# Last four hidden tiles transposed by TensorE, the first rests taken with a negated identity, and every queue reordered

## The reference

```python
def fp4_quant_dequant(x):                  # blocks of 16 along the last dim
    scale = jnp.maximum(jnp.max(jnp.abs(xb), -1, keepdims=True) / 6.0, 1e-12)
    idx = jnp.searchsorted(_MID, jnp.abs(xb / scale))
    return _GRID[idx] * jnp.sign(xb / scale) * scale
gate, y = fp4_linear(x, w_gate), fp4_linear(x, w_up)
h = silu(gate) * y
return fp4_linear(h, w_down)
x = layernorm(x + attn(x)); x = layernorm(x + ffn(x))
```

## Time and profile before

| | us |
|---|---|
| median of 3 runs | 320.72 (320.18 to 323.29) |
| the profiled execution, whole | 319.53 |
| its span, first to last instruction | 317.8 |
| TensorE, VectorE, ScalarE, GpSimd busy | 299.8, 278.9, 223.8, 241.5 |
| mean granted TensorE clock | 0.982 |

### The profile page before, as it was taken

How to read it: one execution, slowest core, us unless ns; L and a number is a source line. 1 busy time by engine, 2 the same in 40 slices (tenths; PEclk the granted TensorE clock), 3 DMA queues, 4 the chain that set the end, 5 groups by cost and what they waited for, 6 DMA issues and landing times.

```text
span 317.8 us, 6470 instructions
## 1 busy us (share of the span) xinstructions
PE 299.8 (94%) x1911; PEld 271.1 (85%) x1911; DVE 278.9 (88%) x725; ACT 223.8 (70%) x545; POOL 241.5 (76%) x258
## 2 busy tenths in 40 slices
PE   6949999999999989999999999999999999999783
PEld 2939988999899879889999998999999998899682
DVE  4996699969999999999988996989998899998953
ACT  7582986679677488669785886686877758587563
POOL 2897886476968967896978889487998757769671
PEclk9996999999999999999999999999999999999979
DMA  6704011832637446433562269338463273267601
GB/s 223 279 35 134 1 68 34 140 74 86 185 75 121 92 86 144 157 95 98 150 180 75 65 107 198 88 104 151 103 120 84 67 112 84 71 136 130 77 33 66
DMA packets 38722, 34.36 MB, mean 108 GB/s; under 512 B 25760, under 2 KB 31776, under 8 KB 38688
## 3 DMA queue, kind: packets, MB, share of 16 engines
q1 hardware_dynamic: 32064, 22.81, 34.5%
q10 hardware_dynamic: 6624, 11.15, 11.1%
HBM read 22.87 MB, written 5.18 MB: 88 GB/s over the span
## 4 chain that ended last, share of the span: by engine, by line
PE 67%; POOL 9%; issue 7%; DVE 7%; DMA 6%; ACT 3%; SPq 1%; ACTq 0%; POOLq 0%; DVEq 0%
PE ps L2160 15%; PE ps L2161 15%; PE ps L2164 15%; PE ps L2173 5%; PE ps L2174 5%; PE ps L2170 5%; DMA h_gT<-h_g 4%; POOL h_q L504 3%; DMA w_pair<-in_w_attn_dram 2%; PE ps L2224 2%; POOL h_n L485 1%; DVE hqT_lo L1584 1%; PE ps L2269 1%; POOL pr_lo L445 1%; PE ps L2283 1%
## 5 line engine op out<-in xcount | busy, mean ns | idle before, releaser
L2160 PE MATMUL ps<-guT_hi,xqT_hi 128*128 128x512 f32 (+1 forms) x192 | 74.0, 385 | 1.5 <-ACT xqT_hi L822 1.4
L2161 PE MATMUL ps<-guT_lo,xqT_hi 128*128 128x512 f32 (+1 forms) x192 | 72.1, 375 | 0.0
L504 POOL TENSOR_TENSOR h_q<-h_gT,h_sT 128x768 f32<-128x768 bf16 x30 | 51.8, 1731 | 12.3 <-DVE hqT_lo L1584 10.7
L2164 PE MATMUL ps<-guT_hi,xqT_lo 128*128 128x512 f32 (+1 forms) x192 | 56.5, 375 | 0.0
L485 POOL TENSOR_TENSOR h_n<-w_raw,h_rs 128x704 f32<-128x704 f32 x32 | 47.1, 1473 | 9.0 <-DVE h_rs L1414 8.9
L2160 PEld LDWEIGHTS ps<-guT_hi,xqT_hi 128*128 128x128 f32 x192 | 36.1, 188 | 6.8 <-ACT xqT_hi L822 1.7
L445 POOL TENSOR_TENSOR pr_lo<-pr,pr_hi 128x512 fp32r<-128x512 f32 (+3 forms) x32 | 28.5, 901 | 16.8 <-ACT pr_hi L791 16.8
L2164 PEld LDWEIGHTS ps<-guT_hi,xqT_lo 128*128 128x128 f32 x192 | 35.5, 188 | 6.0 <-DVE xqT_lo L1521 0.2
L2161 PEld LDWEIGHTS ps<-guT_lo,xqT_hi 128*128 128x128 f32 x192 | 36.1, 188 | 4.5
L2160 PE MATMUL ps<-dnT_hi,hqT_hi 128*128 128x256 f32 x160 | 39.6, 283 | 0.0
L2161 PE MATMUL ps<-dnT_lo,hqT_hi 128*128 128x256 f32 x160 | 39.5, 283 | 0.0
(11 more groups left out here) (130 smaller groups left out, 852.1 us busy)
## 6 DMA issues: line engine op xcount, KB each, us to landing
h_sT<-h_scales_dram SPq DMA_DIRECT2D x30, 384.0 KB
out_dram<-wq_gu ACTq DMA_DIRECT2D x31, 128.0 KB, 1.8
xs<-in_x_rows_dram ACTq DMA_DIRECT2D x7, 512.0 KB, 4.6
x_full<-in_xt_rows_dram ACTq DMA_DIRECT2D x6, 512.0 KB, 3.7
w_raw<-in_w_ffn_dram SPq DMA_DIRECT2D x6, 352.0 KB, 6.0
h_scales_dram<-h_s SPq DMA_DIRECT2D x30, 32.0 KB, 2.6
w_pair<-in_w_attn_dram SPq DMA_DIRECT2D x1, 512.0 KB, 5.1
x_full<-in_xt_rows_dram SPq DMA_DIRECT2D x1, 512.0 KB, 3.5
```

The source lines that it names most:

```text
L504: nc.gpsimd.tensor_tensor(h_q[:, p, :], h_gT[:, p, :, :].rearrange("p c t -> p (c t)"), h_sT[:, p, :], ALU.mult).then_inc(h_quant, 1)
L2160: nc.tensor.matmul(dst, lh, rh, start=(first and i == 0), stop=False)
L2161: nc.tensor.matmul(dst, lh, rl, start=False, stop=False)
L2164: last = nc.tensor.matmul(dst, ll, rh, start=False, stop=(end and i == len(terms) - 1))
```

## The change

Three things. Tiles 28 and 29 take TensorE's way too, so the DMA way ends with tile 27 (the counts in `h_transpose`, `h_round` and `h_divisors` shift by two). The rests of v and of the quantised x of sequence 0 are no longer subtracted on VectorE: TensorE subtracts the high part in PSUM with the negated identity and ScalarE copies the rest. And the five queues are written out in another order, with other banks and other waits for them; the first of sequence 0's scores stand ahead of `combine`.

```diff
-        h_at = {30: (7, 5), 31: (4, 3)}
+        h_at = {28: (7, 6), 29: (7, 3), 30: (7, 6), 31: (7, 3)}
...
+            def v_remainder(n, u):
+                act.wait_ge(v_left, 2 * n + u + 1)
+                c = slice(2 * u, 2 * u + 2)
+                nc.scalar.copy(v_lo[:, c, :].rearrange("p i d -> p (i d)"), ps[:, v_at[n][u], :]).then_inc(v_lo_ready, 1)
...
+            def xq_remainder(n, u):
+                act.wait_ge(xq_left, 2 * n + u + 1)
+                c = slice(D * u, D * (u + 1))
+                nc.scalar.copy(xqT_lo[:, :, c], ps[:, xq_at[n][u], :].rearrange("p (c t) -> p c t", c=DK)).then_inc(xqT_lo_ready, 1)
...
             def v_rest(n, u):
                 dve.wait_ge(v_hi_ready, 2 * n + u + 1)
+                if n == 1 and u == 0:
+                    dve.wait_ge(v_lo_ready, 2)
...
+            def v_subtract(n, u):
+                c = slice(2 * u, 2 * u + 2)
+                pe.wait_ge(v_hi_ready, 2 * n + u + 1)
+                nc.tensor.matmul(ps[:, v_at[n][u], :], neg_ident[:], v_hi[:, c, :].rearrange("p i d -> p (i d)"), start=False,
+                                 stop=True, skip_group_check=True).then_inc(v_left, 1)
...
+            def xq_subtract(n, u):
+                c = slice(D * u, D * (u + 1))
+                pe.wait_ge(xqT_hi_ready, 2 * n + u + 1)
+                nc.tensor.matmul(ps[:, xq_at[n][u], :], neg_ident[:], xqT_hi[:, :, c], start=False, stop=True,
+                                 skip_group_check=True).then_inc(xq_left, 1)
```

More of the change, by code:

```diff
@@ L630, in _ @@
             x_dequant(4, 1)
+            out_stats(9, 1)
+            p_rest(5, 1)
             h_spread(13, 1, 7)
[L632 removed]
+            p_rest(5, 2)
+            h_normalise(16, 0)
+            p_rest(5, 3)
+            h_spread(14, 0, 8)
             x_stats(5, 0)
[L634 to L636 removed]
+            x_rest(6, 0)
+            out_stats(10, 0)
+            x_rest(6, 1)
             x_normalise(5, 0)
[L638 removed]
@@ L2364, in _ @@
-            reads(2, 0, [(v_lo_ready, 5)])
+            reads(2, 0, [(h_grid, 3)])
+            h_scale_rows(3, 1, [(h_grid, 3)])
+            gate_up(5, 1, 1, 0)
+            values(2, 1, [(z_ready, 5)])
+            gate_up(5, 1, 1, 1)
             xq_transpose(1, 1, [(hs_copied, 4)])
@@ L2391, in _ @@
+            scores(2, 3, [(pr_ready, 11)])
+            gate_up(6, 1, 2, 1)
+            h_scale_rows(4, 0, [(pr_ready, 12)])
+            h_scale_rows(5, 1, [(xqT_lo_ready, 4)])
+            pe.wait_ge(wT_lo_ready, 9)
+            down(0, 0, [(wT_lo_ready, 7)])
+            down(1, 1, [(hs_copied, 6)])
+            gate_up(7, 1, 3, 0)
+            reads(2, 1, [(x_grid, 5)])
             gate_up(7, 1, 3, 1)
+            xq_transpose(2, 0, [(z_ready, 6)])
+            scores(3, 0, [(o_ready, 2)])
@@ L2436, in _ @@
-            scores(5, 1, [(o_ready, 9)])
-            h_scale_rows(14, 0, [(pr_ready, 21)])
-            gate_up(15, 3, 3, 1)
-            xq_transpose(4, 0, [(hs_copied, 15)])
-            down(9, 1, [(pr_ready, 22)])
-            reads(5, 0, [(h_grid, 15)])
+            down(7, 3, [(z_ready, 10)])
+            gate_up(15, 3, 3, 1)
+            h_scale_rows(12, 0, [(o_ready, 8)])
+            h_scale_rows(13, 1, [(h_grid, 14)])
+            values(5, 0, [(pr_ready, 21)])
+            h_scale_rows(14, 0, [(hs_copied, 14)])
@@ new lines, in _ @@
+            reads(5, 1, [(v_lo_ready, 12)])
+            h_scale_rows(16, 0, [(h_grid, 17)])
+            down(11, 3, [(h_grid, 17)])
+            scores(6, 0, [(z_ready, 12)])
+            scores(6, 1, [(hs_copied, 17)])
+            h_scale_rows(17, 1, [(h_grid, 15)])
+            gate_up(18, 4, 2, 1)
+            gate_up(19, 4, 3, 0)
+            down(12, 0, [(x_grid, 11)])
+            gate_up(19, 4, 3, 1)
+            xq_transpose(5, 0, [(hs_copied, 18)])
+            h_scale_rows(18, 0, [(h_grid, 18)])
```

2079 lines of the change are left out of this document (1025 added, 1054 removed).

## The result

The changed kernel took 316.19 us in the median (313.95 to 323.64, four runs) against 320.45 us of the kernel before; the ratio is 0.986, 95% interval 0.982 to 0.991. In a second set of runs it took 314.51 us (313.01 to 316.10, six runs) against 320.44, ratio 0.982, 0.977 to 0.987. So it is 1.4 to 1.8% faster. The forecast was 314.8 us.

The account below looks back on a forecast made before the run. TensorE, busy 94% of the span, was taken as the bound, with losses at both ends. Start -1.8, end -4.1, middle 0 sum to -5.9: 319.5 to 313.6 us profiled, 314.8 from the median of 320.7; range 310.5 to 320.5.

Parts of the forecast that it names:

- Start: First scores and values reordered, rests off VectorE: gate_up(0) 3.5 us early; counted as -1.8 us, bounds 0 and -3.5.
- The walk through the queues: Start followed with known durations: reads(0, 1) ends at 19.5 us, x_rest(1, 1) at 23.5, gate_up(0) at 34.7.
- the half of the lead given to the clock: Start: a clock fall between 21.4 and 26.5 us might give back about 3.4 us; half the lead taken, -1.8.
- The row on which I leaned: Kernel before, start: TensorE had 2.0 us of work between 19 and 23.5 us, then ran at half clock.
- End: Tiles 28 and 29 transposed by TensorE: 21.6 us against 25.7, so -4.1 us, bounds -5.1 and -1.
- the forecast's steps: End followed from gate_up(31) at 0: transposes of 28 at 2.8 us, down(31) ends at 19.65.
- the two waits for h_q: End: TensorE waits 0.65 us for h_dequant(30) after down(28), and 0.4 us for h_dequant(31) after down(29).
- what I held against the Trainium skill's rule: End: the trace disagrees that the last two DMA transposes are coverable, with 4.99 and 7.59 us in the chain.
- Middle: All queues reordered, TensorE's middle work the same: 0 us, bounds -3.1 with all gaps gone and +8.
- rival (4): Middle: downs in four bunches; landings of 7.6 to 8.9 us cost about 2.6 each, 10.4 in all, 325 us; chance 0.10.
- the signs that I named: gate_up(0) near 34.7 us; end idle under 1.5 us, no DMA transpose in its chain; middle idle about 3 us.
- signs of being wrong: Middle gaps over 2 us behind L2164 or L2160, a clock under 1 there, or the end's chain through GpSimd.

Follow-up runs that it names:

- the exchange of the ends: The changed kernel with the old end, from about gate_up(29), tiles 28 and 29 on the DMA transposes: 320.96 us, ratio 0.997.
- the transposes first: The changed kernel with the DMA transposes of tiles 8, 9 and 24 to 27 issued ahead of the scale spreads on SyncE's queue: 312.49 us, ratio 0.974.
- narrow spreads: The changed kernel with the scale spreads cut to one sixth of their columns from tile 2 on, output made with stale scales: 310.64 us, ratio 0.969.

## Why the prediction was right, and where it was not

**Start.** The walk through the queues held to within half a us: reads(0, 1) waits only for the ScalarE copy (ends at 17.7 for 17.3), x_rest(1, 1) is there at 23.8 for 23.5, gate_up(0) at 35.03 and 34.67 us for the 34.7 forecast. The step that failed is the half of the lead given to the clock, -1.8 in place of -3.2 to -3.6. In the execution of 323.64 us the clock stayed at 1.00 all through 20 to 29 us. In the other it fell to 0.50 in the same place, at 25 and 26 us:

```profile
25.00:26.00 1.00, 1.00 (x7) 0.50 0.99 385
26.00:27.00 1.00, 1.00 (x6) 0.50 1.07 438
```

and gate_up(0) came only 0.36 us later, of which 0.24 stood already at w_transpose(0) (20.02 for 19.78 us), ahead of the fall. In the execution that held the clock, waits of 0.3 and 0.5 us for ScalarE and VectorE stand between 25 and 27 us; in the other the slower products fill that time. I had priced the half clock as if the stretch were all TensorE's work. The row on which I leaned was also misread: between 19 and 23.5 us the kernel before has 1.6 us of busy time, not 2.0. What I had not seen is that the lead hangs on the order behind it: with the old order from gate_up(2) on it is lost by 66 us, on VectorE's rests of values and of the quantised x.

**End.** Forecast -4.1; the trace gives -3.0, and the exchange of the ends 4.8 with an uncertainty of 2, a longer hole of its own included. From gate_up(31) to the last product it was 19.65 us by the forecast's steps and 20.7 in the trace; of the two waits for h_q of 0.65 and 0.4 us one is there with 0.6, and another 0.6 stands ahead of tile 28's transposes, behind VectorE's h_g. The number was about right for a partly wrong reason. I read "DMA h_gT 7.59" in the chain as the cause. With both transposes landing 2.3 and 3.9 us earlier the wait stayed at 3.2 us, so beside that path ran another, as long: VectorE's divisors of the last tile, h_normalise(31), h_spread(29), h_dequant(30). What the change takes away is h_spread(29) between the two, and the order. That also takes back what I held against the Trainium skill's rule (DMA: Bandwidth & Descriptors, Rules for kernel authors), to issue a DMA early and wait for it late: the last transpose landed at 299.78 us and h_normalise(31) ended at 299.79, so it was covered, if by no more than a hair.

**Middle.** Forecast 0, bounds -3.1 to +8; the trace gives +2.7, the execution of 323.64 us some 7 more. The term was mis-sized, and its mechanism is in its last step that of rival (4), to which I gave 0.10: a transpose that lands after 8.5 us, over the 7.5 from which I had let it decide, stops the chain of the grids at tile 26. What makes the transposes late is not a bunch of downs. GpSimd's h_spread(22), which frees h_gT, runs without a wait of its own behind other work and ends at 260.6 us; on SyncE write_h_scales(26) stands ahead of tile 24's spread and waits for scales that ScalarE has copied at 260.7; then two spreads and two transposes are issued within 4 us. The downs 20 to 22 begin only at 260.5. Rival (4)'s price of 2.6 us for a bunch meets TensorE's gap of 2.5 to 2.7 by luck, since by its own limit a landing 1.0 us too long costs 1.0. Of the four bunches only this one has a gap behind it in the execution of 316.10 us; behind downs 8 to 10 the one of 323.64 us idled for 4.7. Rival (4) took landings as given; the runs show what makes them long here: the spreads' traffic, and a place behind it on the queue.

The Trainium skill states (DMA: Bandwidth & Descriptors, Queues, rings and completion order) that SyncE's transfers share one ring on each of the DMA engines and that each engine takes its descriptors in ring order. The trace agrees: tile 24's transpose lands after 8.5 us behind its spread and after 2.8 ahead of it, with both spreads issued within 3.4 us behind it. Had I read the new order of SyncE's queue with it, the transposes behind a spread in it would have been a term of the sum.

**Sum.** -1.8 - 4.1 + 0 = -5.9 was forecast; the medians give -4.3 and -5.9. In the traces the start was 1.4 us better than its term, the end 1.1 short of it, the middle 2.7 worse: 2.4 us short in all, and the two profiled executions do differ by only 3.4 us. That the second set's median, 314.51 us, falls on the forecast of 314.8 is therefore partly luck: the profiled execution of the kernel before lay 1.2 us under its median, the profiled one of the changed kernel 1.6 over its own.

Of the signs that I named, TensorE's idle time came out as forecast: 1.3 us between gate_up(31) and the last product (under 1.5) and 2.9 in the middle (about 3). But two signs of being wrong came too: a gap over 2 us in the middle, behind L2174, which was L2164 before, and a clock under 1 there. What stays open: why the landings of tiles 8 and 9 went to 12 and 13 us in one execution (with the transposes first, four runs show none of it, which is few), and why one place behind a spread costs 8.5 us and another 5.0.

## What to carry to other kernels

On one DMA queue, put the transfer that a chain waits for ahead of the bulk one, even when both become ready at the same time; here that is six such moves, worth 2.0 us by the medians where the whole change is worth 4.3 to 5.9. When a chain of waits names a DMA, ask what stands in order behind it on the next engine before taking the DMA for the cause; if a second path is as long, shortening the first gives nothing. A lead won at the start is kept only if the order behind it can take it up, so judge the edit with that order, and price a drop of the clock only for the part of the stretch in which the engine is the one awaited.

## What the hardware did that was not expected

- One kind of transfer, a DMA transpose of the same size, landed after 2.7 to 2.8 us ahead of every spread, after 5.0 and 5.5 behind one spread of 384 KB, after 6.9 to 8.8 in the changed kernel's execution of 316.10 us, where two of them are issued close together, and in the one of 323.64 us after 11.9 and 13.2.
- TensorE's clock took two courses over the same instructions and nearly the same gaps at 20 to 29 us: 1.00 throughout in one execution, 0.50 for about 3 us in another. The cost was at most 0.36 us.
- The runs of one kernel differ by the granted clock. The changed kernel took 313.0 to 314.0 us in three runs at 0.998 to 1.00 and 316.0 and 316.1 in two at 0.989. The four runs with narrow spreads all had 0.998 to 1.00 and lie within 0.6 us. Whether the late transfers or the clock make the difference between runs is not shown; the fall at 25 us comes ahead of every late transfer.
